# Bias by columns, sets marked by replacement, another order of the set-up calls, and thirteen of the zero products

## The reference, cut to what matters

```python
# x (8, 256, 256); ctx (8, 64, 256); itok (256, 4) in 0..63; two gates
xn = layernorm(x)                                   # eps 1e-5
q = einsum('bsd,ed->bse', xn, W_q) + b_q
scores = einsum('bse,ne->bsn', q, desc_router) / 16
scores = where(set n is one of the token's 4 sets, scores, -inf)
weights = softmax over the two highest scores, 0 elsewhere      # TOPK = 2
x = x + tanh(g_xattn) * einsum('bsn,bnd->bsd', weights, ctx)
xn = layernorm(x)
gate, up = xn @ Wg.T, xn @ Wu.T                     # (tokens, 2048), Wg, Wu, Wd stored as 4-bit
inter = gelu_tanh(gate) * up                        # codes with one scale per 32
x = x + tanh(g_ffn) * (inter @ Wd.T)
```

## Time and profile before

| | |
|---|---|
| median of three executions | 310.67 us (310.47 to 311.12) |
| the profiled execution's own time | 311.26 us |
| its span, first to last instruction | 309.5 us |
| busy share | PE 98%, PEld 81%, DVE 72%, ACT 50%, POOL 47% |
| granted TensorE clock, mean | 1.000 |

### The profile page before, as it was taken

One profiled execution on the slowest core, in us unless ns is written; L12 is line 12 of the kernel. 1 busy time (PEld: TensorE's weight loads), 2 busy tenths in 40 slices (PEclk: granted clock), 3 DMA queues, 4 the chain that ended last, 5 costly groups with the idle time before them and its releaser, 6 DMA issues.

```text
span 309.5 us, 4648 instructions
## 1 busy us (share of the span) xinstructions
PE 302.0 (98%) x1537; PEld 251.0 (81%) x1537; DVE 223.6 (72%) x478; ACT 155.9 (50%) x287; POOL 144.8 (47%) x138
## 2 busy tenths in 40 slices
PE   6998999999999999999999999999999999999996
PEld 4777888787788788888888888888888888888885
DVE  3999999899985669687676678777676565544545
ACT  3476665657455453435555453444654533444341
POOL 3447455636742342876353325866442233432421
PEclk9999999999999999999999999999999999999999
DMA  6970440020000021326240111424130001110102
GB/s 184 253 186 0 150 124 0 0 37 1 0 2 0 2 34 17 77 57 123 70 101 3 17 17 26 94 53 85 63 94 0 0 15 26 26 40 0 37 0 68
DMA packets 47288, 16.11 MB, mean 52 GB/s; under 512 B 38944, under 2 KB 44448, under 8 KB 47264
## 3 DMA queue, kind: packets, MB, share of 16 engines
q1 hardware_dynamic: 44576, 12.92, 18.0%
q0 software_dynamic: 864, 2.10, 2.5%
q10 hardware_dynamic: 1824, 0.79, 1.1%
HBM read 11.08 MB, written 3.15 MB: 46 GB/s over the span
## 4 chain that ended last, share of the span: by engine, by line
PE 78%; issue 7%; POOL 6%; DVE 4%; ACT 2%; DMA 2%; SPq 0%; DVEq 0%; POOLq 0%
PE ring_ps L1317 49%; PE acc_ps L1351 17%; PE acc_ps L1364 4%; PE att_ps L1364 3%; POOL act_lo L525 3%; POOL w_nat L507 2%; DMA x_sb<-in_x_dram 2%; PE att_ps L1219 1%; POOL w_nat L518 1%; PE ring_ps L1302 1%; ACT act L695 1%; DVE act L1006 0%; DVE act L1000 0%; DVE x_sb L1157 0%; ACT act L691 0%
## 5 line engine op out<-in xcount | busy, mean ns | idle before, releaser
L525 POOL TENSOR_TENSOR act_lo<-act,act_hi 128x512 fp32r<-128x512 f32 x63 | 82.1, 1302 | 118.8 <-ACT act_hi L702 118.6
L1317 PE MATMUL ring_ps<-xt_hi,w_hi 128*128 128x512 f32 (+1 forms) x264 | 103.8, 394 | 1.0 <-ACT xt_hi L675 0.7
L1317 PE MATMUL ring_ps<-xt_hi,w_lo 128*128 128x512 f32 (+1 forms) x264 | 100.9, 384 | 0.0
L1317 PE MATMUL ring_ps<-xt_lo,w_hi 128*128 128x512 f32 (+1 forms) x264 | 100.2, 384 | 0.0
L691 ACT ACTIVATE act<-ring_ps 128x512 f32<-128x512 f32 x64 | 38.1, 596 | 84.2 <-PE ring_ps L1317 83.8
L1000 DVE SCALAR_TENSOR_TENSOR act<-act,ring_ps 128x512 f32<-128x512 f32 x64 | 43.7, 683 | 39.1 <-ACT act L691 38.9
L1006 DVE SCALAR_TENSOR_TENSOR act<-act,ring_ps 128x512 f32<-128x512 f32 x64 | 43.8, 685 | 27.2 <-ACT act L695 25.9
L1317 PEld LDWEIGHTS ring_ps<-xt_hi,w_hi 128*128 128x128 f32 x264 | 49.7, 188 | 11.1 <-issue 1.2
L1317 PEld LDWEIGHTS ring_ps<-xt_lo,w_hi 128*128 128x128 f32 x264 | 49.0, 188 | 10.3 <-DVE xt_lo L938 0.2
L695 ACT ACTIVATE act<-act 128x512 f32<-128x512 f32 x64 | 40.5, 632 | 32.7 <-DVE act L1000 32.7
L1317 PEld LDWEIGHTS ring_ps<-xt_hi,w_lo 128*128 128x128 f32 x264 | 49.8, 188 | 8.3
(11 more groups left out here) (129 smaller groups left out, 331.9 us busy)
## 6 DMA issues: line engine op xcount, KB each, us to landing
x_t<-in_x_dram SPq DMA_DIRECT2D x48, 32.0 KB, 2.1
w_nat<-w_nat SPq DMA_DIRECT2D x96, 16.0 KB
out_dram<-x_sb SPq DMA_DIRECT2D x6, 256.0 KB, 2.2
x_sb<-in_x_dram SPq DMA_DIRECT2D x1, 1024.0 KB, 8.4
ln_dram<-normed SPq DMA_DIRECT2D x16, 64.0 KB, 2.2
w_nat<-ln_dram SPq DMA_DIRECT2D x16, 64.0 KB, 2.0
packed<-L_ffn_gate_W_packed_dram SPq DMA_DIRECT2D x3, 256.0 KB, 2.9
packed<-n_L_ffn_up_W_packed_dram SPq DMA_DIRECT2D x3, 256.0 KB, 3.3
```

The lines of the kernel that those rows point to most:

```text
L525: pool.tensor_tensor(act_lo[:, s % RING, :], act[:, s % ACT_RING, :], act_hi[:, s % RING, :].bitcast(F32), ALU.subtract).then_inc(inter_lo, 1)
L1317: i = pe.matmul(into[:, tok], wt[:, n, w], xt[:, c % 2, k, tok], start=(k, j) == order[0], stop=(k, j) == order[-1])
```

## The change

What the edits do, by engine:

- **Bias.** Instead of spreading b_q over 64 partitions, multiplying it by the router and reducing (two DVE instructions, one product), the kernel loads b_q as two columns of 128 numbers of 4 bytes and PE multiplies these columns, spread by a step of 0, with the turned router: two products ahead of `turn_x(0)`.
- **Sets marked by replacement** (sequences 0 to 3). The lookup of indices, the comparison with a ramp, the weighing and the adding go. DVE negates and sums the top two, fills places 2 to 7 of the top eight with SPARE, and replaces in each half the top two scores by CHOSEN (`match_replace`, over 64 scores and 6 spare places). ACT takes tanh(2 s - first - second) over all 64 scores of each half and adds one; DVE multiplies that by (marked == CHOSEN). The score scale is halved for it.
- **Loads.** The token sets move from POOL's queue to ACT's, second there; b_q becomes the third.
- **Order.** DVE: `input_variance(1)` and `unpack(0, 0)` earlier, `input_stats(CB)` ahead of `rows_low(0)`, `rows_low(1)` ahead of `ln2_low(0)`, `unpack` stages spread. ACT: `lead_out(0)` behind `compact(0)` and the gates' tanh, `rows_high(1)` ahead of `normalise(0)`, `compact(1)` and `compact(2)` together behind `ln2_high(0)`, `x_out(1)` and `rows_high(3)` changed. PE: both `turn_x` and both `score` next to each other, `turn_normed(1)` ahead of the first half of up product 1, `score(2)` from step 2 to ahead of the second half of up product 1.
- **Zero products.** Thirteen at the start stay, thirty go.

```diff
 BANKS = 4
 LAG = 2
-SCORE_SCALE = float(D) ** -0.5
+SCORE_SCALE = 0.5 * float(D) ** -0.5
 assert KT == 2 and HALVES == 2 and UNITS == 16 and P == HALVES * SETS and down_packed.shape[0] == D
...
 pool.iota(iota_i[:, :], [[1, SETS]], base=0, channel_multiplier=0).then_inc(iota_made, 1)
 pool.wait_ge(ident_made, 1)
 pool.affine_select(out=ident[:, :], in_=ident[:, :], compare_op=ALU.not_equal, fill=1.0, base=0,
                    pattern=[[-1, P]], channel_multiplier=1).then_inc(ident_made, 1)
 pool.memset(minus_half[:, :], -0.5).then_inc(minus_half_made, 1)
+pool.memset(scores[:, :, :, SETS:], SPARE).then_inc(spares_made, 1)
 for i, g in enumerate((g_xattn, g_ffn)):
...
-sc.dma_start(bq_sb[:, :], b_q.rearrange("(a d) -> a d", a=1).to_broadcast([SETS, D])).then_inc(small_loaded, 16)
+sc.dma_start(tok_sb[:, :, :], token_sets.rearrange("(p h) k -> p h k", h=HALVES)).then_inc(tokens_loaded, 16)
+sc.dma_start(bq_t[:, :], b_q.rearrange("(k p) -> p k", p=P),
+             allow_slow_non_contiguous=True).then_inc(small_loaded, 16)
 sc.wait_ge(warm_made, 1)
...
+    q = b % CB
     sc.wait_ge(lead_ready, b + 1)
-    for k, factor in enumerate((-0.5, 0.5)):
-        i = sc.activation(lead_tanh[:, b % CB, :, k], lead[:, b % CB, :], ACT.Tanh, scale=factor)
-    i.then_inc(lead_tanh_ready, 1)
+    if b >= BY_ROWS:
+        for k, factor in enumerate((-1.0, 1.0)):
+            i = sc.activation(lead_tanh[:, q, :, k], lead[:, q, :], ACT.Tanh, scale=factor)
+        i.then_inc(lead_tanh_ready, 1)
+        return
+    for h in range(HALVES):
+        i = sc.activation(soft[:, q, h, :], scores[:, q, h, 0:SETS], ACT.Tanh, bias=lead[:, q, h:h + 1], scale=2.0)
+    i.then_inc(soft_made, 1)
+    sc.wait_ge(soft_made, b + 1)
+    sc.activation(soft[:, q, :, :], soft[:, q, :, :], ACT.Identity, bias=1.0).then_inc(lead_tanh_ready, 1)
...
               ACT.Copy, scale=-SCORE_SCALE / D).then_inc(score_w_copied, 1)
 x_t_out(1)
-lead_out(0)
 compact(0)
 sc.wait_ge(gates_loaded, 16 * 2)
 sc.activation(gates[:, :], gates_in[:, :], ACT.Tanh).then_inc(gates_ready, 1)
+lead_out(0)
 sc.wait_ge(gates_ready, 1)
...
               ACT.Copy).then_inc(down_scales_placed, 1)
-compact(1)
 rows_high(0)
+rows_high(1)
 normalise(0)
 probs_out(1)
 ln2_high(0)
-rows_high(1)
+compact(1)
+compact(2)
 x_out(0)
-compact(2)
 down_tile_high(0)
 normalise(1)
 ln2_high(1)
 square(0)
 rows_high(2)
-x_out(1)
 tanh(0)
 square(1)
+x_out(1)
+rows_high(3)
 tanh(1)
-rows_high(3)
 for c in range(CHUNKS):
...
     q = b % CB
     after(("top8", b))
-    dve.tensor_tensor(lead[:, q, :], top8[:, q, :, 1], top8[:, q, :, 0], ALU.subtract).then_inc(lead_ready, 1)
+    if b >= BY_ROWS:
+        dve.tensor_tensor(lead[:, q, :], top8[:, q, :, 1], top8[:, q, :, 0],
+                          ALU.subtract).then_inc(lead_ready, 1)
+        return
+    dve.scalar_tensor_tensor(lead[:, q, :], top8[:, q, :, 0], -1.0, top8[:, q, :, 1],
+                             ALU.mult, ALU.subtract).then_inc(lead_ready, 1)
+    mark(("spares", b), dve.memset(top8[:, q, :, 2:8], SPARE))
 def find_where(b):
     q = b % CB
-    for h in range(HALVES):
-        i = dve.max_index(top8_at[:, q, h, :], top8[:, q, h, :], scores[:, q, h, :])
-    mark(("top8_at", b), i)
-    after(("top8_at", b))
     if b >= BY_ROWS:
+        for h in range(HALVES):
+            i = dve.max_index(top8_at[:, q, h, :], top8[:, q, h, :], scores[:, q, h, 0:SETS])
+        mark(("top8_at", b), i)
+        after(("top8_at", b))
         dve.tensor_scalar(rows_at[:, q, :, :], top8_at[:, q, :, 0:2], b * SETS, None,
                           ALU.add).then_inc(rows_found, 1)
         return
-    mark(("picked", b), dve.tensor_tensor(
-        picked[:, q], iota_i[:, :].unsqueeze(1).unsqueeze(1).to_broadcast([P, HALVES, 2, SETS]),
-        top8_at[:, q, :, 0:2].unsqueeze(3).to_broadcast([P, HALVES, 2, SETS]), ALU.is_equal))
+    if b == 0:
+        dve.wait_ge(spares_made, 1)
+    after(("spares", b))
+    for h in range(HALVES):
+        i = dve.match_replace(marked[:, h, :], top8[:, q, h, :], scores[:, q, h, :], CHOSEN)
+    mark(("marked", b), i)
 def weigh(b):
...
                                                half_gate[:, 0:1], ALU.add, ALU.mult))
         return
-    after(("picked", b))
-    mark(("weighed", b), dve.scalar_tensor_tensor(
-        picked[:, q], lead_tanh[:, q].unsqueeze(3).to_broadcast([P, HALVES, 2, SETS]), 1.0, picked[:, q],
-        ALU.add, ALU.mult))
-    after(("weighed", b))
-    dve.tensor_tensor(probs[:, q, :, :], picked[:, q, :, 0], picked[:, q, :, 1], ALU.add).then_inc(probs_ready, 1)
+    after(("marked", b))
+    dve.scalar_tensor_tensor(probs[:, q, :, :], marked[:, :, 0:SETS], CHOSEN, soft[:, q, :, :],
+                             ALU.is_equal, ALU.mult).then_inc(probs_ready, 1)
 def add_rows(b):
...
                 acc_ps[:, 0, 0:KT * SETS].rearrange("p (k n) -> p k n", k=KT)).then_inc(router_copied, 1)
-dve.wait_ge(small_loaded, 16)
-dve.wait_ge(router_loaded, 16)
-dve.tensor_tensor(bq_sb[:, :], bq_sb[:, :], router_sb[:, :], ALU.mult).then_inc(bias_weighed, 1)
-dve.wait_ge(bias_weighed, 1)
-dve.tensor_reduce(set_bias[:, :], bq_sb[:, :], AXIS.X, ALU.add).then_inc(bias_weighed, 1)
 dve.wait_ge(iota_made, 1)
...
 after("score_bias")
+input_variance(1)
 read_scores(0)
 find_top(0)
 find_lead(0)
+unpack(0, 0)
 find_where(0)
 weigh(0)
-input_variance(1)
-for stage in range(3):
-    unpack(0, stage)
+unpack(0, 1)
+unpack(0, 2)
...
 find_top(1)
 find_lead(1)
@@ -1056,27 +1079,28 @@
 find_where(1)
 find_shift(0)
 weigh(1)
+input_stats(CB)
 rows_low(0)
-unpack(1, 0)
-unpack(1, 1)
+rows_low(1)
 ln2_low(0)
 update_stats(1)
 update_variance(1)
-rows_low(1)
+unpack(1, 0)
 find_shift(1)
+unpack(1, 1)
 unpack(1, 2)
 down_tile_low(0)
 turn_blocks(CB)
-input_stats(CB)
 ln2_low(1)
 input_variance(CB)
-for stage in range(3):
-    unpack(2, stage)
+unpack(2, 0)
 cubic(0)
+unpack(2, 1)
 rows_low(2)
 gated_of(0)
 cubic(1)
 inter_of(0)
+unpack(2, 2)
 gated_of(1)
...
-    pe.wait_ge(bias_weighed, 2)
+    pe.wait_ge(small_loaded, 16)
     pe.wait_ge(router_copied, 1)
-    pe.matmul(acc_ps[:, 0, KT * SETS:(KT + 1) * SETS], set_bias[:, :].to_broadcast([SETS, P]),
-              ident[0:SETS, 0:SETS], start=True, stop=True).then_inc(bias_done, 1)
+    for e in range(KT):
+        i = pe.matmul(acc_ps[:, 0, BIAS_AT:BIAS_AT + SETS],
+                      bq_t[:, e:e + 1].to_broadcast([P, P]), router_t[:, e, :],
+                      start=(e == 0), stop=(e == KT - 1))
+    i.then_inc(bias_done, 1)
...
-warm(15)
+warm(13)
 turn_router()
-warm(8)
+spread_bias()
 turn_x(0)
 fold_router()
-spread_bias()
-warm(2)
+turn_x(1)
 score(0)
-turn_x(1)
-warm(4)
+score(1)
 add_x(0)
-score(1)
-warm(2)
 turn_probs(0)
-warm(4)
 attend_first(0)
 add_x(1)
-warm(4)
 turn_tile(0)
 turn_tile(1)
-warm(4)
 turn_probs(1)
 turn_normed(0)
 attend_first(1)
-first_half, second_half = slice(0, ST), slice(ST, TOK)
-halves = (("gate", 0, gate_done), ("up", 0, up_done), ("gate", 1, gate_done), ("up", 1, up_done))
-for kind, u, _ in halves:
-    if kind == "gate":
-        pe.wait_ge(rows_lo, u + 1)
-    bank_free(kind, u)
-    project(0, u, 0 if kind == "gate" else 1, bank_of(kind, u), first_half, 1)
-    if (kind, u) == ("up", 0):
-        turn_tile(2)
+first_products("gate", 0)
+turn_tile(2)
+first_products("up", 0)
+first_products("gate", 1)
 turn_normed(1)
-for kind, u, done in halves:
-    project(0, u, 0 if kind == "gate" else 1, bank_of(kind, u), second_half, 2).then_inc(done, 1)
-    if (kind, u) == ("gate", 0):
-        turn_tile(3)
+first_products("up", 1)
+second_products("gate", 0, gate_done)
+turn_tile(3)
+second_products("up", 0, up_done)
+second_products("gate", 1, gate_done)
 turn_tile(4)
+score(CB)
+second_products("up", 1, up_done)
...
         elif s >= LAG:
             down_last_chunk(s - LAG)
         for b in next_sequences(c, n, SCORE):
-            score(b)
+            if b > CB:
+                score(b)
         for b in next_sequences(c, n, ATTEND):
```

More of the change, by code:

```diff
@@ L18 @@
 LN_EPS = 1e-5
-MASKED = -3.0e38
+MASKED = -1.0e38
+CHOSEN = 2.0e38
+SPARE = 3.0e38
 GELU_CUBIC = 0.044715
@@ L117, in build_program @@
         router_sb = sb("router_sb", [SETS, D])
+        bq_t = sb("bq_t", [P, KT])
         wq_sum = sb("wq_sum", [P, KT])
-        set_bias = sb("set_bias", [SETS, 1])
         router_t = sb("router_t", [P, KT, SETS])
@@ L141, in build_program @@
         normed = sb("normed", [P, CB, HALVES, D])
-        scores = sb("scores", [P, CB, HALVES, SETS])
+        scores = sb("scores", [P, CB, HALVES, SETS + 6])
         top8 = sb("top8", [P, CB, HALVES, 8])
@@ L148, in build_program @@
         choice = sb("choice", [P, HALVES * 2 * D])
-        picked = choice[:, 0:CB * HALVES * 2 * SETS].rearrange("p (q h k n) -> p q h k n", q=CB, h=HALVES, k=2)
+        soft = choice[:, 0:CB * HALVES * SETS].rearrange("p (q h n) -> p q h n", q=CB, h=HALVES)
```

(26 more changed lines are left out.)

2 lines of the change are left out of this document (removed).

## The result

The changed kernel takes 317.5 us (316.6 to 318.5, 4 runs) against 310.8 (310.5 to 311.1, 4 runs) before: ratio 1.0215, 95% interval 1.0196 to 1.0235. It is 6.7 us slower. I had predicted 310.0 with a range up to 311.3: wrong in sign and far outside the range. Medians and ranges take in all runs of a kernel, ratios only those within 1.5% of its fastest run.

A forecast was written before the change was run, and what follows sets the result against it. PE's stream of products, full from 30 us on, bounds the kernel; time is gained only by starting it earlier. Set-up gains summed to 0.65 to 0.8 us, taken as 0.7: profiled 311.26 to 310.6, median 310.67 to 310.0, range 309.1 to 311.3.

The forecast's parts named there:

- Up to the scores ... I take 0: Start up to x of sequence 0 at 6.99: b_q columns land near 6.5, worth 0, bounds 0 and +2 us.
- slower, by the bias columns: Rival, 8%: columns land at 7.9, `turn_x(0)` is 1.4 us late, total 311.2 us.
- slower, by the clock: Rival, 11%: PE pieces from 7 to about 10.5 us run at half speed, 0.9 us slower, total 311.6.
- gate product 0: After the first set-up steps: claimed to start at about 19.9 us instead of 20.51.
- The thirty missing zero products are worth nothing: Set-up to gate product 0: no gain beyond what is counted, since PE waits in their place.
- in that cover, worth 0: DVE before x of sequence 0 at 6.99: the two bias instructions that go lie under this wait, worth 0.
- The rest: Steps from the scores through gate product 3 and later: a gain of 0.65 to 0.8 us, taken as 0.7.
- the statistics of sequence 2 wait for x: DVE at about 17.0 us: `input_stats(CB)` stands still 0.9 us until x lands at 17.9; bounds 0 and 0.65 lost.
- the idle time of DVE ahead of `unpack(0, 0)`: Sets of sequence 0: DVE idle before `unpack(0, 0)`, as the last packed load lands at 10.0 to 10.6 us.
- the second halves: After `normalise(1)`, 0.57 us earlier: claimed to start at 24.8 us in place of 25.37.
- tile 3: After the second halves: claimed to start at 25.85 us in place of 26.43, gain 0.58.
- gate product 3: Behind `rows_low(4)`, claimed to end at 35.25: gain 0.65 us, bounds 0.15 and 0.8; start near 35.3.

The follow-up runs named there:

- e15: The changed kernel with one edit, the token sets loaded on POOL's queue so the bias columns are second on ACT's: 313.2 us, ratio 1.0066.
- e11: e5 with the token load back on POOL's queue, so the bias columns are second on ACT's: 312.25 us, ratio 1.0046.
- e13: e11 plus two one-element memsets and three already-met waits on DVE, where the bias row was multiplied and added up: 310.8 us, ratio 0.9997.
- e16: e13 with input_stats(CB) where the changed kernel has it: 310.4 us, ratio 0.9991.
- e5: e4 with input_stats(CB) moved back behind turn_blocks(CB): 312.45 us.
- e1: The changed kernel with all 43 zero products back: 316.3 us (312.2 to 318.5, 6 runs); ratio of the three fastest runs 1.0049.
- e4: The changed kernel with all 43 zero products and spread_bias behind fold_router: 312.6 us, ratio 1.0054.
- e6: e4 with the bias row loaded in the old way and the tokens as third load of ACT's queue: 312.5 us (311.6 to 315.3).
- e3: The changed kernel, 13 zero products, with spread_bias moved behind fold_router: 314.5 us, ratio 1.0140.
- e2: The kernel before with only the first 13 zero products: 313.4 us, ratio 1.0109.
- e12: The kernel before with the 23 zero products at the start and behind the router, without the other 20: 311.1 us, ratio 1.0011.
- e14: e16 with 23 zero products in place of 43: 310.3 us, ratio 0.9989.
- e9: e7 with the new order of set-up calls (old bias path, tokens on POOL's queue, all zero products): 310.4 us, ratio 0.9987.
- e7: The kernel before with only the sets marked by replacement: 310.8 us, ratio 1.0003.
- e17: e11 with one more tile of 4 bytes per partition, which no instruction uses: 311.9 us, one run.

## Why the prediction was wrong

The medians step down from 317.5 to 310.4 in this order: 4.3 us with the columns' load moved up (e15), 0.9 with the thirty zero products, the later bias products and the statistics back (e11), 1.5 with the filler instructions (e13), 0.3 with the statistics where the change has them (e16). The first and the third are clear of the noise; the intervals of e15 and e11 overlap, and so do those of e13 and e16. What the columns cost depends on the rest: 4.3 us without the thirty zero products and with the bias products in front (e15), 0.2 with all of them and the bias products late (e5 against e11). With all of them and the bias products in front the runs disagree: those of e1 that its ratio counts have the median of e4, the other three lie some 5 us above.

*"Up to the scores ... I take 0" failed, and most of the miss is this term.* I priced the third load of ACT's queue like the second one of before, 4.7 us, plus its later issue. It took 6.0 and landed at 7.7. My own upper bound was 6.5 and +2 us, and I dropped it because the load carries 1 KB. Between the two small tiles size did not matter: e6's third load is the other tile with four times the bytes and lands as late (6.3), and the same columns as second load need 3.2 us (e11). The place alone is not the whole either, since before 128 KB in third place took 5.2 and 64 KB in fourth 6.6; by the first of these the columns would have landed at 6.9. What makes a small third load land late no run here shows: with its place its issue time moved too, by 0.5 us. The rule of the Trainium skill that I had cited (DMA: Bandwidth & Descriptors, Rules for kernel authors), one descriptor per element, gives no time. Had the single elements been the reason, the columns would have stayed late in e11; they did not, so the trace speaks against it here. The other half of the term was wrong as well: x of sequence 0 is in DVE's hands at 6.00, so the cover that was to end at 6.99 is a microsecond shorter.

*The rival "slower, by the bias columns" had the late landing and a sixth of the price*, 1.2 us over the forecast where the result lies 7.5 over it. It let `turn_x(0)` start 1.4 late; it started 1.64 late (8.63 against 6.99). But I let that delay pass at the normal speed of PE. Behind the wait of 2.9 us the level stays low until the transposes at 22.12; without that wait, in e3 and e15, it is back by 16.2 and 15.8.

*The rival "slower, by the clock" was right in its sign and too small in its length.* Its "against" (PE is busy until 4.4 as before) was the mistake: the thirteen end at 4.0, PE waits 0.36 us for the router, and then for 2.9. It also let the level come back at 10.5 us; it came between 22.1 and 23.5. From the start of `turn_x(0)` to gate product 0 passed 13.5 us before (6.99 to 20.51) and 18.1 after (8.63 to 26.69): beyond the late start, 4.5 us, in which the doubled pieces lie.

*"The thirty missing zero products are worth nothing" failed.* Alone, in the kernel before, they are worth 2.5 us (e2): some 2 for the two at the start and the eight behind the router, 0.4 for the other twenty (e12). Where the columns come second and everything else is mended, the twenty are worth nothing (e14 against e16).

*Two instructions that go from DVE "in that cover, worth 0" failed in a way that no row of before could show.* 1.5 us, by what their going does to VectorE's program, 200 us later (e11 against e13).

*The rest held in the mechanism and gave a third of its size.* With the three causes gone (e9, e16), gate product 0 starts at 19.91 in e9 (forecast 19.9), the second halves at 24.57 (24.8), tile 3 at 25.64 (25.85), gate product 3 at 34.92 (35.3). The replacements take 0.22 us and the statistics of sequence 2 wait for x, 0.81 us (0.9); only the idle time of DVE ahead of `unpack(0, 0)` isn't there, it starts at 10.97 without a wait. Yet the median gains 0.23 us in place of 0.7 (e9), and the marked sets alone nothing (e7). In e9's trace the stream leads that of before by 1.0 us at gate product 3, by 0.86 at 214 us (214.08 against 214.94) and by 0.6 at 235 (234.75 against 235.34): in between the adds of gathered rows, at 213.08, fall under POOL's low half and take 2.70 as in e11. So part of the gain is given back by a collision that an earlier stream triggers. The rest of the gap is in the comparison: the profiled execution of before lay 0.6 us over its median, that of e9 0.25.

What stays open: why the instruction at 200.66 starts late. It recurs at one more product of an activation, 100 us later (300.64 in e11, 0.47 idle), and shows at the same two places of the program in the changed kernel (206.96 and 307.04), whatever the clock had done. The other traces agree: all eight kernels with the bias by columns and no filler have it (the changed one, e1, e3, e4, e5, e11, e15, e17), none of the eleven with the old bias instructions or the filler has it. That ties it to the program and not to the time, and the one run of e17 speaks against the layout of the tiles. Whether the fetching of VectorE's instructions is behind it no run here shows. Nor did I try filler instructions in the changed kernel alone. Open too are why the third small load is late, and what decides whether a run of e1 keeps the level.

## What to carry to other kernels

Price a load from a trace that has one at its place in its queue, and not by its bytes alone; where no such row exists, let the worst of the stretch into the range; ahead of all else put on PE's queue only what waits for nothing. Zero products are no padding where a tensor engine waits for transfers: in this kernel only those among pieces that wait for another engine anyway could go. Let the pieces' own durations, not the clock row, say which level they ran at. If two kernels part ways long after the edit, compare single instructions at the first landmark that differs before looking for a cause in the edit's own data.

## What the runs showed that I had not expected

- A small load (1 or 4 KB) in third place of ACT's queue needs 5.4 to 6.7 us, one in second place 2.8 to 3.5 for the same two tiles. A load of 128 KB needs 4.6 to 5.2 in third place.
- After a wait of 1.46 us (e2) or 2.05 us (e1) TensorE is back at the 1.2 GHz level three or two pieces later; the kernel before waits 1.32 us among its zero products and keeps the 2.4 GHz level. In the changed kernel the pieces are slow until 22 us while the clock row says 1.00.
- An add of VectorE with two inputs in SBUF stands still while POOL works: one of four takes 1.52 us in place of 0.48. The extra 1.0 us fits what is left of POOL's 1.31: in e11 that runs from 202.38 to 203.69, and the adds end at 203.97. The Trainium skill (SBUF — State Buffer, SBUF: two separate sides) says that the two engines share a pair of ports that is locked for a whole instruction, and that the loser blocks; the trace agrees, with this number. Products with one input in PSUM don't show it (L1033 takes 0.69 at 209.34 in e11, beside POOL's low half from 208.71 on).
- Two instructions and the waits with them, gone from the start of VectorE's program, cost 1.5 us some 200 us later.
